# A two-layer attention kernel: in the second layer the causal masks, the sums and the division of a step change engine and place

## What is computed

```
qk = x @ qk_w + qk_b;  q, k = split(qk);  v = x @ v_w          # 16 heads of 8
scores = where(causal, q @ k.T / sqrt(8), -max)
attn = softmax(scores)
uniform = tril(ones / row)                                    # running mean over the tokens so far
new_attn = resid_gain * attn + skip_gain * eye - centre_gain * uniform
out = (new_attn @ v) @ cproj_w
```

## Time and profile before

| | |
|---|---|
| median of 3 runs | 973.65 us (971.24 to 975.08) |
| the profiled execution | 975.81 us, its span 974.0 us |
| PE busy | 780.0 us, 80% of the span |
| DVE busy | 644.7 us, 66% |
| ACT busy | 503.4 us, 52% |
| POOL busy | 414.9 us, 43% |
| first maximum of layer 1 | at 686.5 us of the span |

### The profile page before, as it was taken

The page is one execution under the profiler, slowest core; times in us unless marked ns, Lnnn a source line. Parts: engine busy times, 40 slices in busy tenths (PEclk is TensorE's granted clock), DMA queues, the critical chain, the costliest instruction groups (busy, mean ns, idle before and its releaser), DMA issues.

```text
span 974.0 us, 19905 instructions
## 1 busy us (share of the span) xinstructions
PE 780.0 (80%) x6277; PEld 510.3 (52%) x6278; DVE 644.7 (66%) x1137; ACT 503.4 (52%) x870; POOL 414.9 (43%) x407
## 2 busy tenths in 40 slices
PE   0894796999999999629999999145788989999984
PEld 0752453655555555315555555044566666666663
DVE  6562895898898898515666566373547777676753
ACT  1243253777787776704433334177455555655441
POOL 7006776465656554505777777671201010111000
PEclk9996887999999999859999999666799999999997
DMA  5695744445645542151222221422846465665511
GB/s 144 215 185 135 175 127 116 96 107 119 140 96 127 131 98 63 43 170 43 57 57 54 54 54 46 124 65 56 171 98 157 114 141 137 136 145 131 121 54 51
DMA packets 132670, 106.12 MB, mean 109 GB/s; under 512 B 23317, under 2 KB 124633, under 8 KB 129545
## 3 DMA queue, kind: packets, MB, share of 16 engines
q1 hardware_dynamic: 122348, 91.23, 40.8%
q0 software_dynamic: 4352, 8.99, 3.0%
q10 hardware_dynamic: 5920, 5.24, 1.7%
HBM read 54.60 MB, written 50.03 MB: 107 GB/s over the span
## 4 chain that ended last, share of the span: by engine, by line
PE 30%; DMA 9%; DVE 6%; ACT 4%; issue 4%; SPq 2%; POOL 1%; DVEq 0%; ACTq 0%; POOLq 0%
PE ps L671 8%; DMA od_d<-ev 4%; PE ps L1593 4%; PE ps L692 3%; DVE mx L1297 3%; DMA rec<-od_d 2%; PE ps L673 2%; PE ps L683 2%; PE ps L665 2%; PE ps L1602 1%; ACT rows L893 1%; PE ps L1545 1%; PE ps L1571 1%; PE ps L1543 1%; SPq L1115 1%
## 5 line engine op out<-in xcount | busy, mean ns | idle before, releaser
L1297 DVE TENSOR_REDUCE mx<-ps 128x4 f32<-128x1024 f32 (+1 forms) x224 | 265.9, 1210 | 121.2 <-PE ps L1545 55.9
L1448 ACT ACTIVATE probs<-probs 128x1024 f32<-128x1024 f32 x128 | 131.9, 1053 | 72.3 <-DVE probs L1307 62.4
L1453 ACT ACTIVATE probs<-ps 128x1024 f32<-128x1024 f32 x96 | 96.8, 1023 | 85.2 <-PE ps L1571 57.8
L1219 POOL TENSOR_TENSOR qkr<-qkf,qk 128x512 f32<-128x512 f32 x27 | 31.2, 1156 | 228.1 <-ACT qk L1417 228.1
L1593 PE MATMUL ps<-probs,vpad 128*32 128x256 f32 (+1 forms) x2048 | 121.7, 368 | 8.1 <-ACT probs L1448 7.6
L1247 POOL TENSOR_TENSOR probs<-probs,tabB 128x1024 f32<-128x1024 f32 x42 | 99.3, 2367 | 56.8 <-ACT probs L1460 56.8
L1537 PE MATMUL ps<-tabA,eyeb 128*128 128x512 bf16 x256 | 101.3, 396 | 17.1 <-DMA ks<-parts_d 11.3
L1307 DVE TENSOR_TENSOR probs<-ps,tabB 128x1024 f32<-128x1024 f32 x86 | 100.6, 1214 | 13.4 <-PE ps L1565 13.4
L1539 PE MATMUL ps<-ks,qs 96*128 96x256 bf16 x512 | 101.5, 280 | 0.0
L671 PE MATMUL ps<-qs,probs 128*128 x144 | 81.0, 645 | 1.4
L1593 PEld LDWEIGHTS ps<-probs,vpad 128*32 128x32 f32 x2048 | 56.1, 112 | 49.4 <-issue 22.9
(11 more groups left out here) (227 smaller groups left out, 1519.1 us busy)
## 6 DMA issues: line engine op xcount, KB each, us to landing
parts_d<-qk SPq DMA_DIRECT2D x64, 192.0 KB, 4.4
qs<-parts_d SPq DMA_DIRECT2D x32, 384.0 KB, 5.0
ks<-parts_d SPq DMA_DIRECT2D x32, 384.0 KB, 6.7
parts_d<-qk SPq DMA_DIRECT2D x64, 128.0 KB, 3.3
od_d<-ev SPq DMA_DIRECT2D x64, 128.0 KB
slots_in<-probs SPq DMA_DIRECT2D x1, 4680.0 KB
probs<-slots_in SPq DMA_DIRECT2D x72, 65.0 KB, 1.8
parts_d<-qk SPq DMA_DIRECT2D x64, 64.0 KB, 1.9
```

The source lines that it names most:

```text
L1297: nc.vector.tensor_reduce(mx[:, s.buf(), t, heads[0]:heads[-1] + 1], ring[:, slot].rearrange("p (h n) -> p h n", n=w), AX.X, ALU.max).then ...
L1448: nc.scalar.activation(probs[:, j, :], probs[:, j, :], ACT.Exp).then_inc(exp_done, 1)
L1453: nc.scalar.activation(probs[:, j, :], ring[:, slot], ACT.Exp).then_inc(exp_done, 1)
```

## The change

In layer 1 only (and three small places ahead of it):

- The causal mask of B0 to B3 is no longer a product on TensorE. VectorE adds `maskB` to the diagonal blocks in PSUM, in place (`causal`), and ScalarE's exponential waits for that.
- The residual gain is folded into the value weights `wvs`, the skip gain becomes a column of VectorE's combined operation, the centre gain is folded into `v.share` ahead of the layer. So one product (with `wv1`) serves the skip part and the running mean.
- GpSimd takes the multiply by the inverse (`scale`), the two sums of the running mean (`running_mean`), the final sum with x (`residual`), the copy of a batch's tokens (`tokens`) and the four operations that split the maxima (`parts_gpsimd`).
- The division is spread over one more step: the reciprocal is taken in step k for batch k-3 behind the third maximum (`INVERT` = 3), the multiply and all behind it in step k for batch k-4. The pipeline runs one step longer.
- Positions move: `QK` 1 to 3, `V` 4 to 5, the late values 0 to 2 and 4, the early values 9 to 8, the output projection 10 to 11, ScalarE's copy of the turned maxima ahead of the exponential of B5. The order of SP's transfers changes with it.

```diff
-    LATE = {0: (2, 3, 4, 5)} if layer else {3: (2, 3), 6: (4, 5), 8: (6, 7)}
-    VALUES = {9: (0, 1)} if layer else {12: (0, 1)}
-    SCALE, INVERT, PROJECT = (2, 7, 10) if layer else (9, 15, 11)
-    QK, V, TURN = (1, 4, NU * 2) if layer else (1, 5, 14)
+    INV, DIV = (-3, -4) if layer else (-2, -3)
+    LATE = {2: (2, 3), 4: (4, 5)} if layer else {3: (2, 3), 6: (4, 5), 8: (6, 7)}
+    VALUES = {8: (0, 1)} if layer else {12: (0, 1)}
+    SCALE, INVERT, PROJECT = (None, 3, 11) if layer else (9, 15, 11)
+    QK, V, TURN = (3, 5, NU * 2) if layer else (1, 5, 14)
...
-    A_PART, A_OUT, A_TWO, A_VAL, A_MAX = (2, 0, 4, 4, NU * 2) if layer else (4, 7, 5, 5, 12)
+    A_PART, A_OUT, A_TWO, A_VAL, A_MAX = (3, 4, 4, 4, 10) if layer else (4, 7, 5, 5, 12)
...
+                    if s.has(INV):
+                        outputs_in(s)
                     if s.has(2):
                         parts(s, 0)
+                    if s.has(INV):
+                        inverses_out(s)
                     if s.has(-2):
                         outputs_out(s)
                     if s.has(2):
                         parts(s, 1)
-                    if s.has(-2):
-                        sums_in(s)
-                        outputs_in(s)
+                    if s.has(INV):
+                        inverses_in(s)
                     if s.has(2):
                         parts(s, 2)
                     if s.has(-2):
-                        inverses_out(s)
-                        inverses_in(s)
+                        sums_in(s)
                     if s.has():
                         maxima(s)
...
+            def scale(s):
+                pool.wait_ge(raw_ld, 16 * (s.n(DIV) + 1))
+                pool.wait_ge(rec_ld, 16 * (s.n(DIV) + 1))
+                if s.has(DIV - 1):
+                    pool.wait_ge(y_full, s.n(DIV - 1) + 1)
+                nc.gpsimd.tensor_tensor(on[:], raw[:], rden[:], ALU.mult).then_inc(on_done, 1)
+            def running_mean(s):
+                pool.wait_ge(e_evac, 2 * (s.n(DIV) + 1))
+                nc.gpsimd.tensor_tensor(cum[:], cum[:], v.share, ALU.mult).then_inc(shaped, 1)
+                pool.wait_ge(shaped, 2 * s.n(DIV) + 1)
+                nc.gpsimd.tensor_tensor(on[:], on[:], cum[:], ALU.add).then_inc(shaped, 1)
+            def residual(s):
+                y = yt[:].rearrange("p (c d) -> p c d", c=2)
+                pool.wait_ge(y_evac, s.n(DIV) + 1)
+                nc.gpsimd.tensor_tensor(y, x[:, bass.ds(s.n(DIV) * 2, 2), :], y, ALU.add).then_inc(fin_done, 1)
+            def second_body(s):
+                if s.has(DIV):
+                    scale(s)
+                if s.has():
+                    tokens(s)
+                if s.has(2):
+                    rest_one(pool, nc.gpsimd, s)
+                    rest_two(pool, nc.gpsimd, s)
+                if s.has(DIV):
+                    running_mean(s)
+                if s.has():
+                    parts_gpsimd(pool, s)
+                if s.has(DIV):
+                    residual(s)
...
-                nc.vector.tensor_tensor_scan(cum[:], v.onesT[:], misc[:, T:2 * T], 0.0, ALU.mult, ALU.add).then_inc(e_evac, 1)
-                nc.vector.tensor_tensor(on[:], misc[:, 0:T], on[:], ALU.add).then_inc(e_evac, 1)
-                dve.wait_ge(e_evac, n + 2)
-                nc.vector.tensor_tensor(cum[:], cum[:], v.share, ALU.mult).then_inc(shaped, 1)
-                dve.wait_ge(shaped, n + 1)
-                nc.vector.tensor_tensor(on[:], on[:], cum[:], ALU.add).then_inc(shaped, 1)
+                dve.wait_ge(e_full, s.n(DIV) + 1)
+                if s.has(DIV - 1):
+                    dve.wait_ge(shaped, 2 * (s.n(DIV - 1) + 1))
+                nc.vector.tensor_tensor_scan(cum[:], v.onesT[:], misc[:, 0:T], 0.0, ALU.mult, ALU.add).then_inc(e_evac, 1)
+                dve.wait_ge(on_done, s.n(DIV) + 1)
+                nc.vector.scalar_tensor_tensor(on[:], misc[:, 0:T], cols[:, 5:6], on[:], ALU.mult, ALU.add
+                                               ).then_inc(e_evac, 1)
+            def causal(s, j, slot):
+                dve.wait_ge(full["B"], NU * s.n(-1) + j + 1)
+                diagonal = ring[:, slot].rearrange("p (h n) -> p h n", n=T)[:, :, 0:P]
+                nc.vector.tensor_tensor(diagonal, diagonal, maskB[:].unsqueeze(1).broadcast_to([P, 4, P]), ALU.add
+                                        ).then_inc(masked, 1)
...
-                    act.wait_ge(full["B"], NU * s.n(-1) + j + 1)
+                    if j < 4:
+                        act.wait_ge(masked, 4 * s.n(-1) + j + 1)
+                    else:
+                        act.wait_ge(full["B"], NU * s.n(-1) + j + 1)
...
-                    elif w == T:
-                        if n % 2 == 0:
-                            diagonal = o[:, T * n:T * n + 2 * T].rearrange("p (h t) -> p h t", t=T)[:, :, 0:P]
-                            nc.tensor.matmul(diagonal, eyeb[:], maskB[:].unsqueeze(1).broadcast_to([P, 2, P]),
-                                             start=True, stop=False, skip_group_check=True)
-                        mm = nc.tensor.matmul(at, k, qs[0:MROW + PARTS, b, h, :], start=False, stop=True, skip_group_check=True)
...
-                        nc.tensor.matmul(misc[:, 0:T], v.wvs[:], batch_tokens(s, -3), start=True, stop=True)
-                        nc.tensor.matmul(misc[:, T:2 * T], v.wv1[:, 1, :], batch_tokens(s, -3), start=True, stop=True
-                                         ).then_inc(e_full, 1)
+                        nc.tensor.matmul(misc[:, 0:T], v.wv1[:], batch_tokens(s, DIV), start=True, stop=True).then_inc(e_full, 1)
```

More of the change, by code:

```diff
@@ L528, in _ @@
             pe.wait_ge(copied, 4 + 4 + 13)
-            for k in range(6):
+            for k in range(7):
                 nc.tensor.matmul(ps[:, 2, k:k + 1], rowsp[:, k, :], v.ones[0:1, 0:1], start=True, stop=True)
@@ L1136, in outputs_in @@
             def outputs_in(s):
-                (used_up,) = ahead(s.n(-3) + 1)
-                if s.has(-3):
+                (used_up,) = ahead(s.n(INV - 1) + 1)
+                if s.has(INV - 1):
                     sp.wait_ge(on_done, used_up)
@@ L1143, in inverses_out @@
             def inverses_out(s):
-                done, loaded = ahead(s.n(-2) + 1, 16 * (s.n(-3) + 1))
-                if s.has(-3):
+                done, loaded = ahead(s.n(INV) + 1, 16 * (s.n(INV - 1) + 1))
+                if s.has(INV - 1):
                     sp.wait_ge(rec_ld, loaded)
@@ L1269, in tokens @@
                 nc.gpsimd.tensor_copy(xb[:], xnT[:, bass.ds(s.n() * T, T)]).then_inc(xb_done, 1)
+            def scale(s):
[27 more added lines that the diff above has]
+                    residual(s)
             def body(s):
-                if s.has() and layer == 0 and s.k >= HELP:
+                if s.has() and s.k >= HELP:
                     tokens(s)
@@ L1287, in _ @@
                 ahead_of[1](pool)
-                pool.wait_ge(v.cleared, 4)
-                body(first)
-            emit(pool, body)
+                pool.wait_ge(v.cleared, 5)
+                second_body(first)
+            emit(pool, second_body if layer else body)
         @block.vector
@@ L1381, in body @@
                             add_bias(s, j, U.slot(s.k, pos))
-                    if kind == "A" and j == NU - 1 and s.has() and (layer or s.k < HELP):
+                        elif layer and j < 4:
+                            causal(s, j, U.slot(s.k, pos))
+                    if kind == "A" and j == NU - 1 and s.has() and (layer == 0 and s.k < HELP):
                         maximum_parts(s)
-                    if layer and pos == 6 and s.has(-3):
-                        add_shape(s)
-                    if pos == INVERT and s.has(-2):
+                    if pos == INVERT and s.has(INV):
                         invert(s)
@@ L1392, in body @@
                             rest_two(dve, nc.vector, s)
-                    if pos == PROJECT and s.has(-3):
+                    if pos == PROJECT and s.has(DIV):
                         project(s)
@@ L1468, in store @@
             def store(s):
[L1469 to L1470 removed]
+                act.wait_ge(fin_done, s.n(DIV) + 1)
+                act.dma_start(v.out[bass.ds(s.n(DIV), 1)].rearrange("b (c p) d -> p (b c) d", p=P),
                              yt[:].rearrange("p (c d) -> p c d", c=2)).then_inc(out_st, 16)
             def body(s):
[L1474 removed]
+                if layer == 0 and s.k < HELP and s.has():
                     if s.has(-1):
@@ L1494, in body @@
                         max_rows(s)
-                if layer and s.has(-3):
+                if layer and s.has(DIV):
                     store(s)
```

87 lines of the change are left out of this document (39 added, 48 removed).

## The result

The changed kernel takes **958.66 us** (median of 4 runs, 957.03 to 960.28), the kernel before, beside it on the same chip, 973.72 (971.24 to 975.08): ratio 0.983, 95% interval 0.981 to 0.986. It is faster, as forecast, and inside the range; but of the 24 us forecast 15 came.

A forecast was written before the change was run, and what follows sets the result against it. TensorE's 14.7 us of work plus 2.1 of waits was taken to bound the 16.8 us step; at 14.9, twelve steps give -22.8, the fill -2, the end +2: total -23, so 950 us, range 938 to 966.

The forecast's parts named there:

- 14.7 to 15.3: Second layer, between first maxima: range of step times in us that was to show the prediction right; laid out at 14.9.
- the late second unit: Second pass on TensorE: its second unit starts 1.31 us late, released by a maximum on VectorE; this was to go.
- The short waits before the remaining value product and the output projection: TensorE, new waits in a step: 0.7 us lost before that value product, 0.3 for GpSimd's two sums.
- bounds of 0.60 and 1.21: VectorE's mask sum in PSUM, us each: half and whole of the 128x1024 sum; steps of 14.7 and 16.1.
- the rival of the dear mask: VectorE's mask in PSUM costs 1.4 us or more and bounds the step; slower, 980 us; chance 0.10.
- the rival of the blocking engines: VectorE's masks are held beside GpSimd's subtractions, 0.8 us each, 1.6 a step; 970 us, no change; chance 0.08.
- GpSimd's stretch: Step's end: GpSimd's serial sums and small operations delay the transposition; step 15.2 to 16.0, total 954 to 964 us; chance 0.12.
- "+2": Pipeline's end, after the last reciprocal: GpSimd's slower multiply, two sums and final sum plus hand-overs add 2 us.
- TensorE's "14.7 to 13.4": TensorE's work per second-layer step, in us, falls by eight mask products (0.88) and one value product (0.44).
- 1.3 us of TensorE's work: TensorE, each second-layer step: work falls from 14.7 to 13.4 us as mask products and one value product leave.
- a late multiply: VectorE: the division's multiply, 1.37 us beside GpSimd's subtraction, delays the maximum that TensorE's second unit awaits, 1.31 us late.
- The masks' 0.88: TensorE, second pass: eight mask products of 0.11 us each leave a step.

The follow-up runs named there:

- the experiment with the multiply first: Kernel before with one number changed: the multiply stands ahead of a step's first maximum, not between the second and third; 975.79 us, ratio 0.999.

## Why the prediction was right, and where it wasn't

**Right: sign, size of the step, prices.** The step is 14.65 against 14.9, a hair under the "14.7 to 15.3" that was to show it right; the late second unit is gone and VectorE's work is 11.33 us against 11.5. The short waits before the remaining value product and the output projection, the last of those signs, are not in the list of waits. The mask in PSUM costs 0.699, where I took 0.69 between bounds of 0.60 and 1.21; with that the rival of the dear mask is out. GpSimd's operations of 128x256 cost 0.72 against my 0.65, within the bound of 0.75. Nothing is held: 64 masks within 686 to 700 ns and 16 combined operations within 457 to 461, beside a GpSimd that is busy 6.54 us a step. That takes the rival of the blocking engines out, and agrees with the Trainium skill, page "SBUF — State Buffer", section "Who interferes with whom", that a VectorE instruction with at most one SBUF input, outside the two-port modes, doesn't contend with GpSimd. GpSimd's stretch does not set the step's end either: between 742 and 888 us no wait for the fourth small operation is listed.

**Failed: the end, "+2".** It was +8.4, and an end that grows by more than 5 us is one of the prediction's own signs of being wrong. The time fell into the range all the same, because the twelve steps gave 2.6 more than forecast and the range reaches 16 above the 950. What I costed, the way behind the last reciprocal, came out at 2.2. Three terms were missing: the drain (3.9, shown by adding one GpSimd operation to the kernel before), the last store of outputs behind the raw load (1.6; the text names that load as moved into the later step, and doesn't ask what stands behind it once no further batch comes; it stays with the multiply on VectorE), and 0.8 ahead of the outputs' copy, whose cause stays open. The drain was in the trace of before, hidden at 902 us, and I did not look for it.

**Failed in its working: TensorE's "14.7 to 13.4".** The run with the product put in again has the products of the kernel before, hardly a wait, and 15.23 a step. So the work before was about 15.2, and its stand 1.6 and not 2.1; the waits listed there, 11.3 at the second unit, 2.6 at the transposition and 0.8 of small ones in nine steps, say the same. After, it is about 15.2 - 0.92 - 0.40 = 13.9, and the stands are some 0.7 where I laid out 1.5. Two errors of opposite sign made the 14.9: that it came so close is luck.

**Failed: what the gain is made of.** I put it down to 1.3 us of TensorE's work and a late multiply. The masks' 0.88 brought 0.26 a step, and nothing in the total. The multiply held by GpSimd does make the 1.3 us wait, as I wrote, but taken out of the way alone it brought nothing: the wait for the division's transfer, for which the prediction has no term in the old step, stood right behind it (9.2 us in nine steps). The one product's 0.44 was right (0.40). Of the 1.99 us between the old step and 14.79, the product is 0.40 and the split of the late values 0.63, each measured at the new order. If these add up, the remaining 0.96 lies with the other positions (the multiply's among them), the additional step of the division and the token copy together. The multiply moved and the division a step longer are the pair that the experiment with the multiply first points to; they were not tried apart from the rest, so which of them it is stays open.

So the change is a good order and a set of engine moves that give back more than they bring: masks, sums and maxima on other engines win 0.14 a step against the kernel with all three back (1.2 us in the twelve steps profiled), and lose 8.3 us in the end: 958.66 against 950.85 us, 0.983 against 0.974.

## What to carry to other kernels

Split a change that moves work and reorders it, and time the order alone: here it is worth more than the whole, and the move that looks largest in busy time (the masks) is worth nothing in the whole time with the new order and costs 7% with the old. Cost the end of a pipeline as its own stage, by what each engine does last and what then still stands behind it. Before believing that an operation's wait sets the step, move that operation alone, and read which wait then stands in its place.

## What the runs showed of the hardware

GpSimd's closing drain takes 6.1 to 8.2 us in the four traces shown here, and starts with its last operation; it cost nothing where another engine worked on that long, and 4 us where GpSimd finished last. TensorE's granted clock was 0.56 over a stretch of 3.24 us, near the lower level, right after TensorE had stood 1.45 and 2.07 us, in the old order with the masks moved; in the other kernels it was 1.00 from 770 to 885 us. In-place sums of VectorE on a PSUM slot, 128x512, cost 0.699 us, against 0.689 for one that reads PSUM and writes SBUF.
